# 3x3 weights in three column pieces, first column and first parameters in small DMAs, score matmuls inside the first convolution

## The reference

```python
x_top    = conv1x1(xn, w_top,    b_top)      # 128 -> 16 channels
x_center = conv1x1(xn, w_center, b_center)   # 128 -> 16 channels
x_bottom = conv3x3(xn, w_bottom, b_bottom)   # 128 -> 128
sp_map = einsum('bnp,bpm->bnm', x_center, x_top)              # 256 x 256 scores an image
sp_map = softmax(sp_map.reshape(b, -1))                        # over a whole image
sp_map = einsum('bnm,bmc->bnc', sp_map, x_bottom).reshape(b, c, h, w)
x = x + conv3x3(xn + sp_map, w_out, b_out)
```

## Time and profile before

| | |
|---|---|
| median of 3 runs | 405.79 us |
| lowest, highest | 405.54, 407.99 us |
| profiled execution, first to last instruction (span) | 405.0 us, 5142 instructions |
| TensorE matmul busy | 381.8 us |
| VectorE, ScalarE, GpSimd busy | 262.8, 290.2, 153.3 us |
| mean granted clock of TensorE | 0.985 |

### The profile page before, as it was taken

The page is one execution under the profiler, slowest core; times in us unless marked ns, Lnnn a source line. Parts: engine busy times, 40 slices in busy tenths (PEclk is TensorE's granted clock), DMA queues, the critical chain, the costliest instruction groups (busy, mean ns, idle before and its releaser), DMA issues.

```text
span 405.0 us, 5142 instructions
## 1 busy us (share of the span) xinstructions
PE 381.8 (94%) x1667; PEld 275.9 (68%) x1667; DVE 262.8 (65%) x570; ACT 290.2 (72%) x516; POOL 153.3 (38%) x126
## 2 busy tenths in 40 slices
PE   8899889989999999999999999999999999988992
PEld 2588666444647677777787767877777768655782
DVE  1846356974241875496864995757957497677774
ACT  5352345935121877987989889999899998887881
POOL 3370000820067629030476773121233366332343
PEclk9999999999699999999999999999999999999997
DMA  7950000000000042903020013043030002120231
GB/s 248 462 188 1 2 0 2 1 0 0 2 1 0 2 136 76 385 30 105 28 52 26 2 50 82 28 144 115 4 129 28 27 26 80 53 78 0 105 109 51
DMA packets 10731, 28.90 MB, mean 71 GB/s; under 512 B 1086, under 2 KB 2238, under 8 KB 10448
## 3 DMA queue, kind: packets, MB, share of 16 engines
q1 hardware_dynamic: 10704, 28.58, 20.3%
HBM read 27.95 MB, written 0.62 MB: 71 GB/s over the span
## 4 chain that ended last, share of the span: by engine, by line
PE 65%; DVE 16%; ACT 15%; issue 3%; POOLq 0%; POOL 0%; ACTq 0%; DVEq 0%
PE ps L421 16%; PE ps L422 15%; PE ps L423 15%; ACT hidh L1064 4%; ACT ps L1065 4%; PE ps L428 3%; PE ps L722 2%; PE ps L433 2%; DVE hidl L1426 2%; PE ps L661 2%; ACT rstd L951 1%; DVE bot L1343 1%; ACT rstd L953 1%; PE ps L444 1%; DVE small L1342 1%
## 5 line engine op out<-in xcount | busy, mean ns | idle before, releaser
L1426 DVE TENSOR_TENSOR hidl<-ps,hidh 128x512 fp32r<-128x512 f32 x160 | 108.2, 686 | 52.8 <-ACT ps L1065 51.2
L392 POOL TENSOR_TENSOR x<-x,parts 128x512 f32<-128x512 f32 x43 | 55.9, 1301 | 151.1 <-DVE parts L1436 99.7
L421 PE MATMUL ps<-xh,wh_all 128*128 128x512 f32 x160 | 74.3, 465 | 2.2 <-DVE hidl L1426 1.7
L1064 ACT ACTIVATE hidh<-ps,par 128x512 fp32r<-128x512 f32 x96 | 68.2, 710 | 8.4 <-PE ps L423 6.4
L421 PE MATMUL ps<-hidh,wh_all 128*128 128x512 f32 (+1 forms) x162 | 64.3, 397 | 4.1 <-DVE hidl L1426 3.8
L1065 ACT ACTIVATE ps<-ps,par 128x512 f32<-128x512 f32 x96 | 65.5, 682 | 0.0
L422 PE MATMUL ps<-hidh,wl_all 128*128 128x512 f32 (+1 forms) x162 | 63.4, 391 | 0.0
L422 PE MATMUL ps<-xh,wl_all 128*128 128x512 f32 x160 | 63.4, 396 | 0.0
L423 PE MATMUL ps<-hidl,wh_all 128*128 128x512 f32 (+1 forms) x162 | 63.1, 390 | 0.0
L423 PE MATMUL ps<-xl,wh_all 128*128 128x512 f32 x160 | 63.0, 394 | 0.0
L382 POOL TENSOR_TENSOR wl_all<-wa,wh_all 128x512 fp32r<-128x512 f32 x40 | 51.2, 1297 | 3.5
(11 more groups left out here) (252 smaller groups left out, 591.4 us busy)
## 6 DMA issues: line engine op xcount, KB each, us to landing
scores_all<-rows_scratch SPq DMA_DIRECT2D x48, 256.0 KB, 3.3
wa<-in_moe SPq DMA_DIRECT2D x2, 4096.0 KB, 16.3
wa<-in_moe SPq DMA_DIRECT2D x1, 2048.0 KB, 9.2
dft_x<-in_dft_x SPq DMA_DIRECT2D x1, 640.0 KB
dft_o<-in_dft_o SPq DMA_DIRECT2D x1, 640.0 KB
w<-in_w_bottom SPq DMA_DIRECT2D x1, 576.0 KB, 7.2
w<-in_w_out SPq DMA_DIRECT2D x1, 576.0 KB, 8.9
cst<-in_consts SPq DMA_DIRECT2D x1, 512.5 KB, 8.0
```

The source lines that it names most:

```text
L392: pool.tensor_tensor(half(x, h), half(x, h), parts[:, n % 2, :], ALU.add).then_inc(s["state_added"], 1)
L421: pe.matmul(o, wh, xhi, start=start, stop=False)
L1064: act.activation(hidh[:, n % 2, f, :], sums, func, bias=bias).then_inc(s["hidden_hi_act"], 1)
L1426: dve.tensor_tensor(hidl[:, n % 2, f, :], bank(sums_bank(n, f)), f32(hidh[:, n % 2, f, :]), ALU.subtract).then_inc(s["hidden_lo"], 1)
```

## The change

It does six things.

1. The 3x3 weights lie in memory by kernel column (dx, then dy) and not by row, so the index is `t * C`, and a kernel column is 384 neighbouring columns (`COLUMN`).
2. The parameters come in two DMAs: the first 68 columns (the biases and the two projections) early, the rest after `w_bottom`.
3. `w_bottom` comes in two DMAs: the first kernel column, then the two others.
4. GpSimd splits a kernel column at a time; the convolution waits for the columns one by one (`split_done`, `dx + 1`).
5. VectorE makes the first low part ahead of the biases of `cen`, and the others in turn with them.
6. The two dummy matmuls go. The score matmuls stand in the bottom convolution ahead of group (0, 3); `turn_max` moves from (0, 6) to (0, 8), `spread_max` from (0, 7) to (1, 1), `turn_bottom(0)`, `sum_exp(0)`, `mix(0)` from (1, 2), (1, 3), (1, 4) to (1, 3), (1, 4), (1, 5).

```diff
+FIRST_PARAMS = PARAM["gate_w"][0]
+COLUMN = 3 * C
...
-            sp.dma_start(par[:], dram["params"]).then_inc(s["params_loaded"], 16)
-            sp.dma_start(w33[:, 0], dram["w_bottom"]).then_inc(s["wb_loaded"], 16)
+            sp.dma_start(par[:, 0:FIRST_PARAMS], dram["params"][:, 0:FIRST_PARAMS]).then_inc(s["first_params_loaded"], 16)
+            sp.dma_start(w33[:, 0, 0:COLUMN], dram["w_bottom"][:, 0:COLUMN]).then_inc(s["wb_loaded"], 16)
+            sp.dma_start(w33[:, 0, COLUMN:], dram["w_bottom"][:, COLUMN:]).then_inc(s["wb_rest_loaded"], 16)
+            sp.dma_start(par[:, FIRST_PARAMS:], dram["params"][:, FIRST_PARAMS:]).then_inc(s["params_loaded"], 16)
...
+            def split_column(which, dx, done):
+                cols = slice(dx * COLUMN, (dx + 1) * COLUMN)
+                split(w33h[:, which, cols], w33l[:, which, cols], w33[:, which, cols], done, 3 * which + dx + 1)
 
             pool.wait_ge(s["wb_loaded"], 16)
-            split(w33h[:, 0], w33l[:, 0], w33[:, 0], s["wb_split"], 1)
+            split_column(0, 0, s["wb_split"])
+            pool.wait_ge(s["wb_rest_loaded"], 16)
+            split_column(0, 1, s["wb_split"])
+            split_column(0, 2, s["wb_split"])
             pool.wait_ge(s["norm_lo"], 2)
             pool.wait_ge(s["wo_loaded"], 16)
-            split(w33h[:, 1], w33l[:, 1], w33[:, 1], s["wo_split"], 2)
+            for dx in range(3):
+                split_column(1, dx, s["wo_split"])
             pool.wait_ge(s["we_loaded"], 16)
-            split(weh[:], wel[:], we[:], s["we_split"], 3)
+            split(weh[:], wel[:], we[:], s["we_split"], 7)
...
-            pe.wait_ge(s["params_loaded"], 16)
+            pe.wait_ge(s["first_params_loaded"], 16)
...
                         if dy == 0:
+                            pe.wait_ge(split_done, dx + 1)
...
-                        w = (3 * dy + dx) * C
+                        w = t * C
...
-            keep_clock(2, 5)
-            scores()
-            pe.wait_ge(s["wb_split"], 1)
-            conv33(0, xph, xpl, s["shift_hi"], s["shift_lo"], s["norm_hi"], s["norm_lo"], 0, s["bottom_done"],
-                   between={(0, 6): turn_max, (0, 7): spread_max,
-                            (1, 2): lambda: turn_bottom(0), (1, 3): lambda: sum_exp(0), (1, 4): lambda: mix(0)})
+            conv33(0, xph, xpl, s["shift_hi"], s["shift_lo"], s["norm_hi"], s["norm_lo"], 0, s["bottom_done"], s["wb_split"],
+                   between={(0, 3): scores, (0, 8): turn_max, (1, 1): spread_max,
+                            (1, 3): lambda: turn_bottom(0), (1, 4): lambda: sum_exp(0), (1, 5): lambda: mix(0)})
...
-            dve.wait_ge(s["params_loaded"], 16)
-            for h in range(2):
+            dve.wait_ge(s["first_params_loaded"], 16)
+
+            def center_half(h):
                 dve.wait_ge(s["proj_done"], 2 * h + 2)
...
-            for dx in range(3):
-                shift_low(0, dx)
+            shift_low(0, 0)
+            center_half(0)
+            shift_low(0, 1)
+            center_half(1)
+            shift_low(0, 2)
...
             mix_half(0)
+            dve.wait_ge(s["params_loaded"], 16)
             shift_weights(0)
...
-        "w_bottom": a["L0_conv_w_bottom"].transpose(1, 2, 3, 0).reshape(C, 9 * C),
-        "w_out": a["L0_conv_w_out"].transpose(1, 2, 3, 0).reshape(C, 9 * C),
+        "w_bottom": a["L0_conv_w_bottom"].transpose(1, 3, 2, 0).reshape(C, 9 * C),
+        "w_out": a["L0_conv_w_out"].transpose(1, 3, 2, 0).reshape(C, 9 * C),
```

More of the change, by code:

```diff
@@ L82 @@
 SIGNALS = [
-    "x0_loaded", "x1_loaded", "params_loaded", "norm_consts_loaded", "consts_loaded", "wb_loaded", "wo_loaded", "we_loaded", "dft_loaded", "rows_stored", "scores0_in", "scores1_in", "scores2_in", "scores3_in",
+    "x0_loaded", "x1_loaded", "first_params_loaded", "wb_rest_loaded", "params_loaded", "norm_consts_loaded", "consts_loaded", "wb_loaded", "wo_loaded", "we_loaded", "dft_loaded", "rows_stored", "scores0_in", "scores1_in", "scores2_in", "scores3_in",
     "moe1_loaded", "moe2_loaded", "moe3_loaded", "stored",
@@ L458, in _, with conv33 @@
                     last.then_inc(s["proj_done"], 1)
-            def conv33(which, hi, lo, early_hi, early_lo, hi_done, lo_done, n0, done, halves=(0, 1), between={}):
+            def conv33(which, hi, lo, early_hi, early_lo, hi_done, lo_done, n0, done, split_done, halves=(0, 1), between={}):
                 for h in halves:
@@ L574, in early_gates @@
                 gate_tiles((4, 5))
-            pe.wait_ge(s["wo_split"], 1)
-            conv33(1, xph, xpl, s["mix_shift_hi"], s["mix_shift_lo"], s["mix_hi"], s["mix_lo"], 0, s["out_conv_done"], halves=(0,),
+            conv33(1, xph, xpl, s["mix_shift_hi"], s["mix_shift_lo"], s["mix_hi"], s["mix_lo"], 0, s["out_conv_done"], s["wo_split"], halves=(0,),
                    between={(0, 2): lambda: turn_bottom(1), (0, 3): lambda: sum_exp(1), (0, 4): lambda: mix(1)})
@@ L582, in _ @@
             pe.wait_ge(s["normed"], 3)
+            pe.wait_ge(s["params_loaded"], 16)
             gate_tiles(range(4))
```

## The result

The changed kernel takes 408.24 us (median of 22 executions, 405.74 to 412.86) against 405.74 for the kernel before (22 executions). The ratio of the two is 1.0058, with a 95% interval of 1.0039 to 1.0078: slower by 2.35 us (1.6 to 3.2). The forecast was 406.8 in a range of 404.3 to 408.0: the sign and the place were right, the size was too small and the range too narrow by 0.2 us.

The account below looks back on a forecast made before the run. The start of mix(1), with TensorE and VectorE both just in time, was taken to bound the kernel. An earlier convolution, outweighed by low parts meeting wel, put mix(1) 1.0 us later: 405.8 + 1.0 = 406.8 us, range 404.3 to 408.0.

Parts of the forecast that it names:

- Loads: Weight loads at the start: first column of w_bottom in before 8.45, the rest at 8.9, between bounds 8.45 and 9.9.
- Columns: GpSimd's weight splits: cast 0.51 and subtraction 1.00, 1.58 us a column; w_out's split and wel become 0.9 us later.
- First low part and S: VectorE takes its first low part at 10.40; S, the first convolution's start, is taken as 11.6, against 14.50 before.
- Scores: Score matmuls inside the first convolution cost TensorE 1.0 us; maximum's spread comes 8.25 and mix(0) 12.1 after the convolution's start.
- GpSimd's start tied to the maximum: GpSimd starts on w_out 1.99 us after the maximum's spread, at 21.85, so not earlier than before.
- The meeting: Mixed half's low parts meet GpSimd's wel in full; the third ends at 31.95, not 30.95, making mix(1) 1.0 us later.
- the clock's term: TensorE's new wait of some 2.9 us before mix(1): no clock fall expected, so nothing added to the forecast.
- Rival D: Clock falls in TensorE's new wait before mix(1): up to 3 or 5 us more, 409.8 or above; chance 0.05.
- The order: Mixed half: first low part passes before wel, the others after; third ends at 31.95, or 32.1 in the other order.
- The sum: Whole kernel: mix(1) starting 1.0 us later moves the end by +1.0, from 405.8 to 406.8.
- Against the median: Whole kernel: the median of the runs, 405.79, lies 0.8 above the profiled span of 405.0; the shift is added to it.
- Rival B: Mixed half: GpSimd and VectorE don't meet, so 1.3 us are gained, giving 404.5; chance 0.17.

Follow-up runs that it names:

- e1: Changed kernel with GpSimd's split of the experts' weights held back until the first half of x1 is written: 405.13 us, ratio 0.9988 to the kernel before.
- e2: Changed kernel with GpSimd's split of w_out moved ahead of its wait for the last low part of xp: 404.57 us, ratio 0.998 to the kernel before.
- e4: Kernel before, with w_out split in three pieces of 384 columns instead of one of 1152: 406.18 us, ratio 1.0011.
- e5: Changed kernel's loads and column splits alone, with the order of the kernel before on TensorE and VectorE: 405.34 us, ratio 0.999 to the kernel before.
- e3: Changed kernel with ten dummy matmuls in TensorE's wait before the output convolution: 406.0 us, ratio 1.003 to the kernel before.
- e10: Changed kernel with w_out split early, steps from turned maximum to mix(0) one group earlier, eight dummy matmuls in the wait for x: 402.7 us, ratio 0.9921.
- e11: Kernel before, with eight dummy matmuls in TensorE's wait for x: 404.64 us, ratio 0.9992.
- e8: Changed kernel's loads and column splits with the old TensorE and VectorE order, and w_out split early: 405.36 us, ratio 0.9997 to the kernel before.

## Why the prediction was right or wrong, point by point

- **Loads: right.** First column at 6.87 (bound 8.45), the rest before 8.47 (I took 8.9).
- **Columns: right.** 0.50 and 1.00 a column (0.51 and 1.00); `wel` ends 8.09 after GpSimd's start on `w_out` (22.85 to 30.94), where it was 7.36: 0.73 more, against 0.9. A column takes 1.53 from start to start (22.85 to 27.45 for three), not 1.58.
- **First low part and S: right.** It was held to 1.16 us by column 2 (the third), and the convolution started 2.38 after the projections, which with the start of before (9.31) is 11.7; I took 11.6.
- **Scores: right**, 1.1 against 1.0. The spread comes 8.52 after the convolution's start (8.25), `mix(0)` 12.39 (12.1).
- **GpSimd's start tied to the maximum: right**, 1.99 after the spread (20.86 to 22.85), as before.
- **The meeting: right in kind, place and size.** It is shown by taking it away (e1, e2: 2.8 and 3.2 us by the ratios, with what hangs on it) and by a dose (e4, e5: 0.7 between the two mixings). In e3, where the clock held, `mix(0)` is 1.05 earlier (forecast 1.2) and the distance between the mixings 2.05 longer (forecast 34.7 - 23.7 = 11.0, so 2.2); what is left is 1.17 in the stretch and 1.2 by the ratio, and the forecast said 1.0.
- **The step that failed** is the clock's term, which the sum put at nothing: "for a wait of this length the rows are for it not happening". Rival D had a chance of 0.05, and it happened, though smaller than I priced it (3 or 5 us). In the profiled execution of the changed kernel the granted clock is 0.51 from 32.7 to 36, and `mix(1)` starts 1.30 behind VectorE's copy where 0.13 would do: 1.2 us late. The copy itself starts 10.11 after `mix(0)`, as forecast (33.9 - 23.7 = 10.2), so what is wrong behind it is the clock alone. Filling the wait (e3) is worth 1.1 us by the ratios, with intervals that overlap; the mean clocks (none of 22 above 0.994, 5 of 12 in e3) speak for it too (from different sets of executions), and say nothing of its size.
- **Why the clock's term was put at nothing:** I argued that a wait of 1.90 had left the clock at 1.00. That row ends with the wait, and the fall comes behind it. In that trace the clock did hold behind it as well, up to 55 us, but it was one execution: in the set of 35 of the kernel before the mean clock goes from 0.981 to 0.997, and behind waits as long as this one six of ten traces have a fall. One trace cannot tell that a wait is harmless.
- **The order: wrong, at no cost to the sum of VectorE's part.** I let the first low part pass ahead of `wel`, 0.15 us before it. With 0.73 and not 0.9 for the columns, both were ready at 28.57, and `wel` went ahead of all three: "In the other order 32.1". The end of the third low part hardly depends on it, as I said: 8.16 after `mix(0)`, where the two orders give 8.25 and 8.4. But "TensorE waits some 2.9 us there", at `mix(1)`, was wrong with it: the *first* low part is late too, and TensorE waits for it in one piece, 2.12 us, at the first group of the output convolution, with the groups up to `mix(1)` behind the wait. Whether the forecast order would have spared the clock was not tried.
- **The sum:** by the ratios, +2.35 us for the changed kernel and +1.2 for e3. So +1.2 is the meeting less what the early start gains, as forecast at 1.0, and about 1.1 is the clock, forecast at nothing; e1 and e2, with neither, are at -0.5 and -0.8.
- **Against the median:** I took the profiled span plus 0.8 as the median. The timed values lie 2.1 above the spans (412.86 and 410.7), so the profiled execution of before (span 405.0) was itself, by this estimate, some 1.4 us above the median. As the shift was added to the median, this changed nothing.
- **Rival B, "the two don't meet", 404.5:** e2 is this rival built, and gave 404.57. But its stretch is 0.6 shorter and not 1.3, and at an equal clock (0.997) it has 404.07 against 404.19 of before, so the number was right in part by luck. The missing 0.7 of the stretch can be read: the convolution starts 2.62 after the projections and not 2.29 (its first low part is held to 1.40), `mix(0)` 12.39 after that and not 12.10, and from `mix(1)` to the centring are 9.05 and not 8.89.

What stays open: why one wait is followed by a fall and the next, as long, is not (1.94 us in e4 and e8). Falls were changed by filling waits, in e3 and e10; the length of a wait as such was not varied. And who goes first when GpSimd and VectorE ask at the same time was seen twice, both times GpSimd, at 28.57 and, in e3, at 28.23.

## What to carry to other kernels

Before making one engine earlier, list what other engines do at its new time on whatever they share: here a stage that started 2.8 us earlier met in full a GpSimd subtraction of which it had met only the last 0.25 us, and lost more than it had gained, the slower clock behind the new wait included. Give an early start to the engine that sits idle (GpSimd had 11 us), not to the one that will wait anyway. And price a new wait of TensorE by the half clock that can follow it, not by its length only; filling it with matmuls that compute nothing gave 1.1 us (e3) and 1.8 us (e10) back by the ratios, both with overlapping intervals, and 0.3 in e11, which is within the noise. A filled wait, an early split and steps one group earlier together made a kernel 3.2 us faster than the one before the change.

## What the runs showed of the hardware

- A VectorE subtraction with both inputs in SBUF that meets a GpSimd one ends 0.61 us after it, in the changed kernel as in the one before; it works the other way as well: GpSimd's cast of 0.50 took 1.03 and its subtraction of 1.00 took 1.49 behind VectorE (e2).
- When GpSimd is held between two VectorE instructions it gets in between them, and the other way round: e2's rows alternate (12.37, 13.81). A back-to-back row of three low parts took 3.74 instead of 2.10 against a GpSimd that was at work all the time (e8).
- TensorE's clock went to the 1.2 GHz level (0.51) one microsecond *after* a wait of 2.12 us had ended, while matmuls ran back to back, and so the work behind the wait paid. Behind waits of 1.90 to 2.06 us six of ten traces have such a fall (0.57 to 0.64 over 4 us), and equal lengths are in both groups. Between executions of the same kernel the number of falls differs, and with it the time: 405.74 us at a mean clock of 0.994 and 412.86 at 0.976.
